# Fused masked attention of a graph layer on one core: seven score products per pair from the third row pair on instead of the fourth, with the key forms, sums and small VectorE work rearranged to suit

## The reference

```
h     = relu(layernorm(x))                       # x: 4096 x 256, f32
lQ    = masked_x @ Wlq ; lK = h @ Wlk ; lV = h @ Wlv + blv
local = where(adj, lQ @ lK.T / 16, -1e9)         # 4096 x 4096, adj: bool
glob  = (masked_x @ Wgq) @ (mean(h) @ Wgk).T / 16
es    = masked_x @ Wes
p     = softmax over the 4096 local scores, glob and es together
res   = p_local @ lV + p_glob * (mean(h) @ Wgv + bgv) + p_es * (masked_x @ Wev + bev)
out   = x + maximum(res, masked_x)
```

## Time and profile before

| what | value |
|---|---|
| median of 3 runs | 729.88 us (729.72 to 729.95) |
| the profiled execution, whole | 730.02 us |
| its span, first to last instruction | 728.2 us |
| TensorE matmuls busy | 722.5 us, 99% |
| VectorE busy | 566.3 us, 78% |
| ScalarE busy | 532.3 us, 73% |
| GpSimd busy | 432.9 us, 59% |
| mean granted TensorE clock | 0.999 |

### The profile page before, as it was taken

One profiled execution on the slowest core, in us unless ns is written; L12 is line 12 of the kernel. 1 busy time (PEld: TensorE's weight loads), 2 busy tenths in 40 slices (PEclk: granted clock), 3 DMA queues, 4 the chain that ended last, 5 costly groups with the idle time before them and its releaser, 6 DMA issues.

```text
span 728.2 us, 15018 instructions
## 1 busy us (share of the span) xinstructions
PE 722.5 (99%) x5248; PEld 512.6 (70%) x5248; DVE 566.3 (78%) x1347; ACT 532.3 (73%) x709; POOL 432.9 (59%) x300
## 2 busy tenths in 40 slices
PE   9999999999999999999999999999999999999998
PEld 7667566667666777776767676676777776676787
DVE  6975988777877788878887887878878787877645
ACT  6884967858677776776878687678767777777690
POOL 4779889455565465556545655566556545644584
PEclk9999999999999999999999999999999999999999
DMA  9784877879779888988978797989888798887796
GB/s 301 131 175 84 158 152 155 155 139 211 158 159 178 166 163 146 214 151 175 170 166 161 157 201 137 195 158 179 171 170 161 150 206 150 178 170 179 135 183 152
DMA packets 364620, 121.93 MB, mean 167 GB/s; under 512 B 324736, under 2 KB 364544, under 8 KB 364544
## 3 DMA queue, kind: packets, MB, share of 16 engines
q1 hardware_dynamic: 364000, 120.44, 82.0%
q10 hardware_dynamic: 544, 0.52, 0.2%
HBM read 36.57 MB, written 4.19 MB: 56 GB/s over the span
## 4 chain that ended last, share of the span: by engine, by line
PE 87%; issue 4%; POOL 3%; DVE 3%; ACT 1%; DMA 1%; DVEq 0%; POOLq 0%; ACTq 0%
PE ps_u L1126 13%; PE ps_u L1128 13%; PE ps_u L1130 13%; PE ps_x L1025 7%; PE ps_x L1024 7%; PE ps_x L1023 7%; PE ps_q L947 4%; PE ps_v L1023 3%; PE ps_v L1025 3%; PE ps_v L1024 3%; POOL p_base L621 2%; PE ps_w L1023 2%; PE ps_w L1025 2%; PE ps_w L1024 2%; PE ps_q L1192 1%
## 5 line engine op out<-in xcount | busy, mean ns | idle before, releaser
L621 POOL TENSOR_TENSOR p_base<-s,p_base 128x1024 f16<-128x1024 f32 x112 | 241.8, 2159 | 228.9 <-ACT p_base L824 228.6
L1126 PE MATMUL ps_u<-v_rows,pT_base 128*128 128x256 f16 x944 | 257.3, 273 | 0.0
L1130 PE MATMUL ps_u<-v_rows,pT_base 128*128 128x256 f16 x944 | 257.3, 273 | 0.0
L1128 PE MATMUL ps_u<-v_rows,pT_base 128*128 128x256 f16 x944 | 257.3, 273 | 0.0
L787 ACT ACTIVATE bias<-adj,big 128x1024 f32<-128x1024 uint8 x127 | 156.5, 1236 | 130.7 <-DVE bmax L1495 128.5
L800 ACT ACTIVATE s<-s,negm,invc 128x1024 f32<-128x1024 f32 x128 | 157.0, 1226 | 8.9 <-DVE negm L1551 8.9
L824 ACT ACTIVATE p_base<-s 128x1024 f16<-128x1024 f32 x122 | 128.9, 1057 | 4.8 <-POOL p_base L621 1.0
L1128 PEld LDWEIGHTS ps_u<-v_rows,pT_base 128*128 128x128 f16 x944 | 92.4, 98 | 52.0
L1126 PEld LDWEIGHTS ps_u<-v_rows,pT_base 128*128 128x128 f16 x944 | 92.4, 98 | 52.0
L1495 DVE CUSTOM_DVE_ANT_0 s<-ps_x,bias 128x512 f32<-128x512 f32 x128 | 87.2, 686 | 48.2 <-PE ps_x L1025 44.7
L1130 PEld LDWEIGHTS ps_u<-v_rows,pT_base 128*128 128x128 f16 x944 | 92.4, 98 | 10.6
(11 more groups left out here) (242 smaller groups left out, 1292.2 us busy)
## 6 DMA issues: line engine op xcount, KB each, us to landing
adj<-adj SPq DMA_DIRECT2D x64, 256.0 KB, 3.2
pT_base<-p_base SPq DMA_TRANSPOSE x234, 3.2
s<-x SPq DMA_DIRECT2D x7, 512.0 KB, 7.7
f32q<-mx SPq DMA_DIRECT2D x14, 256.0 KB, 3.6
xm<-x SPq DMA_DIRECT2D x14, 256.0 KB, 3.1
xm<-mx SPq DMA_DIRECT2D x14, 256.0 KB, 3.5
out<-t_sb SPq DMA_DIRECT2D x14, 256.0 KB, 2.6
mxT_f<-mxT SPq DMA_DIRECT2D x4, 256.0 KB, 3.1
```

The costliest lines, as they stand in the source:

```text
L621: nc.gpsimd.tensor_tensor(p_rows(u)[:, 1], s32[:, p % NS, u % 2], p_rows(u)[:, 0], ALU.subtract).then_inc(s_plo, 1)
L1126: nc.tensor.matmul(acc, turn[:, 0, j], v_rows[:, kc, 0:D], start=opens, stop=False, skip_group_check=True)
L1128: nc.tensor.matmul(acc, turn[:, 0, j], v_rows[:, kc, D:2 * D], start=False, stop=False, skip_group_check=True)
L1130: done = nc.tensor.matmul(acc, turn[:, 1, j], v_rows[:, kc, 0:D], start=False, stop=end, skip_group_check=True)
```

## The change

The constant PC goes from 12 to 8, so pairs 8 to 11 (row pair 2) are done in seven products too; `q_low`, `q_high`, `q_form` and `transpose_q` follow PC and handle that row pair's query in seven forms. The two key sums of groups 0 and 1 move from pair 10 to pair 6 (PC - 2); those of groups 2 and 3 are now one each in pairs 8 and 10, with their own waits, and the low half of T3 of group 3 is written in pair 11. VectorE writes the probabilities' low halves of units 0 to 3 only (0 to 9 before); units 4 to 9 go to GpSimd. GpSimd builds the forms of keys 1 together in pair 4, and those of keys 2 and 3 one per pair in pairs 6 to 8 and 9 to 11. On VectorE the units of masked x (`mx_units`) are split from its scale (`mx_scale`), and in pair 7 they and two subtractions come behind the blocks; from pair 8 on `row_max`, `weights` and the low half of Wev come ahead of block 11 of the pair, `side_rows` and `q_row_scales` too; only `local_rows` stays behind it.

```diff
     NPER = NP * NG
-    PC = 12
+    PC = 8
+    LOWS = 4
     QH = 3
...
         def low_on_dve(u):
-            return u // 2 + LAG_E < PC - 2
+            return u < LOWS
 
...
                     finish(n)
-                if p in (4, 6, 8):
-                    keys_t1(p // 2 - 1)
-                    keys_t2(p // 2 - 1)
-                if p in (5, 7, 9):
-                    keys_t4((p - 3) // 2)
+                if p == 4:
+                    keys_t1(1)
+                    keys_t2(1)
+                    keys_t4(1)
+                if p in (6, 9):
+                    keys_t1(p // 3)
+                if p in (7, 10):
+                    keys_t2(p // 3)
+                if p in (8, 11):
+                    keys_t4((p + 1) // 3 - 1)
             pool.wait_ge(s_xm_end, 32)
...
                 act.wait_ge(s_t3sum, g + 1)
+                act.wait_ge(s_t1, g + 1)
+                act.wait_ge(s_p7, PC - NG + g + 1)
                 nc.scalar.activation(plain(g, 0, 1, 0), ps_q[:, g % 2].rearrange("p (j q) -> p j q", q=P), ACT.Copy
...
                     p_high(u + 1)
-                if p in (PC - 2, PC):
-                    keys_t3_high(p - PC + 2)
-                    keys_t3_high(p - PC + 3)
+                if p == PC - 2:
+                    keys_t3_high(0)
+                    keys_t3_high(1)
+                if p in (PC, PC + 2):
+                    keys_t3_high(p // 2 - 2)
                 if p % NG == 3 and QH <= (p + 5) // NG < NP:
...
                 if n == PC // NG + 1:
-                    pe.wait_ge(s_t3, NG)
+                    pe.wait_ge(s_t3, 3)
                 if n >= QH:
...
                 if g < 2:
-                    pe.wait_ge(s_qf, PC - 3)
+                    pe.wait_ge(s_qf, 7)
                 else:
-                    pe.wait_ge(s_c2, 2)
+                    pe.wait_ge(s_qf, 2 * g + 3)
+                    pe.wait_ge(s_t3, g)
                 for k, (c, hl) in enumerate(((1, 0), (1, 1), (0, 0), (0, 1))):
...
                 if n == 0:
-                    pe.wait_ge(s_t3, 2)
+                    pe.wait_ge(s_t3, NG)
                 if n < QH:
...
                     p_times_v(p, 4, 6)
-                    if p == PC:
-                        keys_t3_sum(2)
-                        keys_t3_sum(3)
+                    if p in (PC, PC + 2):
+                        keys_t3_sum(p // 2 - 2)
                     if p == NPER:
...
                                         ALU.bitwise_and, ALU.bitwise_xor).then_inc(s_mscale, 1)
+
+            def mx_units(n):
+
+                k = n - QH + 1
+                dve.wait_ge(s_mcl, k)
                 nc.vector.tensor_scalar(mpow[:, :].bitcast(I32), mcl[:, :].bitcast(I32), 0x7F800000, None,
...
                     side_top(1)
-                if p == 7:
-                    dve.wait_ge(s_gev, 5)
-                    nc.vector.tensor_tensor(gv_b[:, :], gv_b[:, :], blv_b[:, :], ALU.subtract).then_inc(s_gev, 1)
-                    nc.vector.tensor_tensor(bev_b[:, :], bev_b[:, :], blv_b[:, :], ALU.subtract).then_inc(s_gev, 1)
                 u = 2 * (p - LAG_E)
...
                         p_low(u)
+                    if step == 3:
+                        mx_scale((p + 5) // NG)
                     out11(p)
...
                         p_low(0)
-                    if step == 3:
-                        mx_scale((p + 5) // NG)
                     if project:
...
                         q_row_scales(m)
-                    if p == 8:
-                        row_max(1)
                     if p == 5:
...
                     if p == 7:
+                        mx_units(QH)
                         weights_low()
-                    if p == 9:
-                        wev_low()
-                    if step == 1 and p >= 9:
-                        weights((p - 9) // NG)
-                    if step == 2 and p >= 10:
-                        side_rows((p - 10) // NG, 0)
-                        side_rows((p - 10) // NG, 1)
-                    if step == 3 and p >= 11:
-                        es_rows((p - 11) // NG)
-                        local_rows((p - 11) // NG)
+                        dve.wait_ge(s_gev, 5)
+                        nc.vector.tensor_tensor(gv_b[:, :], gv_b[:, :], blv_b[:, :], ALU.subtract).then_inc(s_gev, 1)
+                        nc.vector.tensor_tensor(bev_b[:, :], bev_b[:, :], blv_b[:, :], ALU.subtract).then_inc(s_gev, 1)
                 else:
                     done = (p - 9) // NG
-                    ended = done < NP - 1
+                    ended = 0 <= done < NP - 1
                     if wino(old):
...
                         add22(p)
+                    if p == PC + 3:
+                        keys_t3_low(3)
                     if project:
...
                         mx_scale((p + 5) // NG)
+                        mx_units((p + 5) // NG)
                     if step == 0 and p >= 12 and p != NPER:
...
                         keys_t3_low(2)
-                        keys_t3_low(3)
                     if wino(old):
...
                         mx_scale((p + 5) // NG)
+                        mx_units((p + 5) // NG)
                     if step == 3 and ended:
                         es_rows(done)
-                    if p < NPER:
-                        out11(p)
                     if project:
...
                         row_max(n)
+                    if p == 9:
+                        wev_low()
                     if step == 1 and ended:
                         weights(done)
+                    if p < NPER:
+                        out11(p)
                     if step == 3 and ended:
```

## The result

The changed kernel takes 735.12 us (734.88 to 735.36) where the kernel before took 729.88: 1.0072 times as long, 95% interval 1.006 to 1.0084. I had forecast 729.3 and a range up to 731.9. The span of the profiled execution went from 728.2 to 733.4.

What follows compares the result with a forecast made beforehand. TensorE was taken as the bound, unbroken from 66 us but for one hole. From the profiled 730.02: -2.6 matmuls, -1.07 hole, +2.6 +0.3 +0.2 stalls gave 729.4, 729.3 against the median; range 727.2 to 731.9.

Steps and rivals of the forecast that it cites:

- The work removed: Pairs 8 to 11 lose three 512-column matmuls each on TensorE, 12 x 0.215: 2.6 us less.
- the time line without waits: Starts of pairs 7 to 13 if no new wait arises: pair 7 at 88.14, pair 13 at 152.2, before 154.84.
- The chain through GpSimd: Low halves waiting for ScalarE and VectorE delay form 2 of keys 3 to 136.4: 2.6 us stall at product 6, pair 11.
- my 133.8: The time at which product 6 of pair 11 was due, 4.2 us behind the pair's start, needing form 2.
- the stalls at pairs 8 and 10: Pair 8: late first add, 0.2 us; pair 10: product 5 waiting for block 12 of pair 9, counted inside product 6's stall.
- Form 4: Form 4 of keys 3, behind masked x on GpSimd, stalls product 4 of pair 11 by 0.1 to 1.1, taken as 0.3 us.
- my sign that VectorE's load was mis-sized: The stated test: more than 1 us lost on TensorE before 130 would mean VectorE's load was mis-sized.
- All stalls of the mechanism: The stalls priced in pairs 8 to 11: +2.6, +0.3 and +0.2 us.
- Elsewhere the order is off TensorE's path: Apart from the hole at 219, reordering VectorE's extras costs nothing, as block 11's bank is wanted 3.9 us later than block 12's.
- the old hole: TensorE's wait at 219 in the kernel before, 1.07 us, which side rows ahead of block 11 were to remove.
- My slower rival: VectorE overloaded in pair 9, block 12 at 124 or later, form 2 at 138.5 or later: 732.7 us, chance 0.17.
- a new hole behind pair 13 would make the sum wrong: The stated test: behind pair 13 nothing was priced except the hole of 1.07 us at 219.

Runs made afterwards that it cites:

- experiment 10: Experiment 9 with units 4 to 7 on VectorE, masked x loaded first, forms 1 and 4 of keys 3 a pair earlier on GpSimd: 729.29 us, 0.9991.
- experiment 3: The changed kernel with eleven idle 512-column matmuls ahead of product 6 of pair 11: 733.37 us, 1.0049.
- experiment 1: The kernel before with only the new order, VectorE's extras ahead of block 11 from pair 12 on: 732.22 us, 1.0028.
- experiment 2: The changed kernel with the old order, block 11 back ahead of the extras: 732.24 us, 1.0035.
- experiment 7: The kernel before with only the second pair of side rows ahead of block 11: 729.22 us, 0.9991.
- experiment 8: Experiment 1 with the load of masked x ahead of the query's transposition on SP: 729.07 us, 0.9991.
- experiment 5: Experiment 2 with form 2 of keys 3 right behind form 1 in pair 9 on GpSimd: 736.60 us, 1.0087.
- experiment 9: Experiment 5 with VectorE's extras of pairs 8 and 9 moved later, and side rows alone ahead of block 11: 734.82 us, 1.0069.
- experiment 6: The changed kernel with the edits of experiments 4 and 5 and block 11 ahead of the extras: 733.11 us, 1.0045.
- experiment 4: The changed kernel with the low halves of units 4 to 9 back on VectorE: 736.37 us, 1.0087.

## Why the prediction was wrong, step by step

**The work removed** (-2.6) and **the time line without waits** were right: experiment 10, with 3.2 us of holes by count, closes to 0.1 us with it. Pair 7 began at 87.85, 0.3 us ahead of my 88.14.

**The chain through GpSimd** was right in its mechanism and its places, and mis-sized. It was to end between 135.1 and 138.4, and I took 136.4. It ended at 137.75. The timelines of GpSimd, ScalarE and VectorE in the changed kernel are these:

```profile
113.38 2.13 POOL L622 TENSOR_TENSOR p_base<-s,p_base 128x1024 f16<-128x1024 f32 x1 [2.43 <-ACT p_base L830]
116.68 2.13 POOL L622 TENSOR_TENSOR p_base<-s,p_base 128x1024 f16<-128x1024 f32 x1 [1.17 <-ACT p_base L830]
...
126.93 2.13 POOL L622 TENSOR_TENSOR p_base<-s,p_base 128x1024 f16<-128x1024 f32 x1
...
136.60 1.15 POOL L566 TENSOR_TENSOR hW<-tw,hW 128x512 f16<-128x512 f32 x1
```

```profile
109.75 1.24 ACT L793 ACTIVATE bias<-adj,big 128x1024 f32<-128x1024 uint8 x1 [4.30 <-DVE bmax L1510]
...
123.09 1.24 ACT L793 ACTIVATE bias<-adj,big 128x1024 f32<-128x1024 uint8 x1 [3.54 <-DVE bmax L1510]
```

```profile
117.32 1.51 DVE L1433 TENSOR_SCALAR invc<-rpow 128x2 f32<-128x2 f32 x1
118.75 1.20 DVE L1438 TENSOR_SCALAR big<-cq 128x2 f32<-128x2 f32 x2
...
122.31 0.68 DVE L1510 CUSTOM_DVE_ANT_0 s<-ps_v,bias 128x512 f32<-128x512 f32 x1
```

Mask bias 19 starts at 109.75 (I had 108.1 to 109.2), mask bias 21 at 123.1 (the late end, 123), because the extras of pair 9 took 4.4 us from 117.32 to block 11 and were again held by GpSimd. From the low half of unit 9 on GpSimd has no idle time: it starts at 116.7 (I had 114.9 to 116.0), and the stretch up to the low half of unit 10, which I had at 9.5 us, takes 10.3. Form 2 itself takes 4.4 us (133.34 to 137.75), unstretched. Product 6 of pair 11 is thus 4.1 us behind my 133.8, near the late end of 1.3 to 4.6; the middle was the wrong choice. That its own hole is 2.57 us where I had 2.6 is chance, since mine was to hold pair 10's as well. The lateness is 0.54 + 1.18 + 2.57 = 4.3, so the stalls at pairs 8 and 10 do lie inside it, as I had it. Form 4 (0.37) was as forecast (0.3). More than 1 us was lost before 130 (0.54 and 1.18), which was my sign that VectorE's load was mis-sized. All stalls of the mechanism came to 4.66 where I took 3.1: 1.6 of the 5.8 us by which the time was missed.

**A term was missing: the clock.** I priced a stall by its length alone. The sum had no price for what TensorE's clock does behind a standstill; it was 1.7 us (experiment 3).

**"Elsewhere the order is off TensorE's path" was the step that failed**, together with the range that rested on it. I had looked only at the bank that block 11 frees. The extras stand ahead of block 12 in either order, but put ahead of block 11 they start earlier, meet GpSimd's low halves and take longer, and block 11 then comes between them and block 12 (experiment 1). So block 12 is late, and behind it the mask bias, the high halves, the query's low half and the load of masked x on SP, which goes out 22.8 us behind the projection instead of 21.3. The row top waits for the load, and lands among GpSimd's low halves. In the changed kernel VectorE's timeline in such a pair reads

```profile
310.02 0.69 DVE L1479 TENSOR_REDUCE mmax<-f32q 128x2 f32<-128x512 f32 x1 [1.57 <-DMA f32q<-mx]
310.74 1.29 DVE L1481 TENSOR_SCALAR mcl<-mmax 128x2 f32<-128x2 f32 x1
...
312.34 2.06 DVE L1495 TENSOR_TENSOR mu<-mpow,unw 128x4 f32<-128x4 f32 x1
...
314.93 0.67 DVE L1510 CUSTOM_DVE_ANT_0 s<-ps_x,bias 128x512 f32<-128x512 f32 x1
```

and GpSimd's beside it

```profile
309.87 2.13 POOL L622 TENSOR_TENSOR p_base<-s,p_base 128x1024 f16<-128x1024 f32 x1 [2.95 <-ACT p_base L830]
312.25 2.13 POOL L622 TENSOR_TENSOR p_base<-s,p_base 128x1024 f16<-128x1024 f32 x1 [0.25 <-ACT p_base L830]
```

A multiplication of four numbers per partition (0.16 us elsewhere) ends at 314.40, when GpSimd's low half ends (314.38). Block 21, behind it, frees the bank of product 1 at 315.6, which was due at 315.39. The Trainium skill ("SBUF — State Buffer", section "SBUF: two separate sides") has the port pair that the two engines share locked for a whole instruction, against VectorE's instructions with two SBUF inputs among others; this is such a one, and these rows agree with it. The later holes are 2.7 us, where I had 0: 2.4 at these places and 0.34 left of the old hole. Experiments 1, 2, 7 and 8 put the 2.4 on the order, and on the load as its carrier.

So the missed 5.8 us are 1.6 of the stalls' size, 1.7 of clock and 2.7 of late holes, 6.0 by this count, 0.2 too many. My slower rival named the mechanism of pair 9 and got 732.7. Its condition wasn't met (block 12 of pair 9 left at 123.0, not 124 or later, and form 2 was out at 137.75, not 138.5), and it lacked the same two terms. Of "a new hole behind pair 13 would make the sum wrong" the condition came true.

## What to carry to other kernels

Where one engine is unbroken, price a change by following each producer's queue to the product it feeds, and where every link waits for the one before, give the late end its weight: here the chain ended near it. Moving work off a loaded queue doesn't help an item that stands behind a waiting one: here six low halves fewer left the form as late as before, and the form ahead of them made the low half late. A reorder "off the path" needs its effect followed through every queue up to the next load, not only the buffer it frees. Small VectorE work on SBUF operands lasted up to ten times as long here (2.1 us for 0.16) where GpSimd was busy, so where it is moved to matters. And a stall of some microseconds on TensorE is to be priced with the half-speed stretch that may stand behind it.

## What the runs showed of the hardware

The clock isn't a function of one hole's length in these runs. In the profiled executions it fell behind standstills of 2.57, 5.28 and 3.55 us (changed kernel, experiments 5 and 9) and of 2.19 us at 114 in experiment 6, and stayed at 1.00 behind 2.11 in experiment 2 and behind 2.09 and 2.35 in experiment 4. Each fall was to 1.2 GHz and lasted 3 us or more. Nor is it fixed by the kernel. In experiment 4 the profiled execution alone kept 1.000 (735.36 us); the other three show 0.997 and took 736.3 to 736.8. In experiment 2 one of five shows 0.998 and took 733.5, the others, at 0.999 to 1.000, 731.9 to 732.3. What decides I can't say: I varied nothing by itself but the filling of the hole (experiment 3), and those other executions have no trace.

VectorE's instructions with an operand in PSUM kept their time beside GpSimd: in the changed kernel all 256 blocks and all 168 adds took 0.66 to 0.69 us. A multiplication of 128x2 numbers in SBUF (L1416 of the kernel) took 0.16 to 2.08 us.
